# Turning the rounded rows of batches 1 to 7 by VectorE blocks and transfers instead of TensorE

## The reference

```python
def _quant_per_tensor(x):
    scale = max(max(abs(x)), 1e-6) / 127
    return round(x / scale), scale

def _qlinear(x2d, w, b):
    xq, sx = _quant_per_tensor(x2d)
    wq, sw = _quant_per_tensor(w)
    return (xq @ wq.T + b) * (sw * sx)

x = x + tanh(g_xattn) * attention(layernorm(x), ctx)
h = gelu(_qlinear(layernorm(x), w1, b1))      # 512 -> 2048
x = x + tanh(g_ffn) * _qlinear(h, w2, b2)     # 2048 -> 512
```

## Time and profile before

| | |
|---|---|
| median of 3 runs | 369.76 us (368.94 to 369.95) |
| the profiled execution: its own time | 368.73 us |
| its span | 366.9 us |
| TensorE matmuls busy | 349.0 us (95%) |
| VectorE busy | 330.2 us (90%) |
| ScalarE busy | 285.2 us (78%) |
| GpSimd busy | 119.8 us (33%) |
| DMA | 84.78 MB, mean 231 GB/s |

### The profile page before, as it was taken

How to read it: one execution, slowest core, us unless ns; L and a number is a source line. 1 busy time by engine, 2 the same in 40 slices (tenths; PEclk the granted TensorE clock), 3 DMA queues, 4 the chain that set the end, 5 groups by cost and what they waited for, 6 DMA issues and landing times.

```text
span 366.9 us, 6644 instructions
## 1 busy us (share of the span) xinstructions
PE 349.0 (95%) x2406; PEld 245.9 (67%) x2418; DVE 330.2 (90%) x630; ACT 285.2 (78%) x493; POOL 119.8 (33%) x178
## 2 busy tenths in 40 slices
PE   6979989999999888999999999999999999999995
PEld 4667767887886775554545455454548888888884
DVE  3698999999999978999999988987769999999996
ACT  1465879889886965879859988789799999999520
POOL 2644578778689790069000000421000000000000
PEclk9869999999999999999999999999999999999999
DMA  7999978565311463767748760000191999995225
GB/s 222 378 404 403 401 278 280 196 228 216 117 37 80 145 203 128 290 268 312 290 200 341 319 260 0 1 2 0 51 409 56 383 395 424 424 422 233 102 116 229
DMA packets 22963, 84.78 MB, mean 231 GB/s; under 512 B 2129, under 2 KB 11857, under 8 KB 14482
## 3 DMA queue, kind: packets, MB, share of 16 engines
q1 hardware_dynamic: 22272, 83.89, 59.2%
q10 hardware_dynamic: 658, 0.46, 0.4%
HBM read 54.99 MB, written 29.36 MB: 230 GB/s over the span
## 4 chain that ended last, share of the span: by engine, by line
PE 60%; DVE 19%; ACT 10%; issue 5%; DMA 3%; POOL 2%; SPq 1%; DVEq 0%; ACTq 0%; POOLq 0%
PE PS L1460 19%; PE PS L1415 17%; PE PS L1257 7%; DVE hmax L1042 7%; PE PS L1318 6%; ACT ring L703 5%; DMA X<-in_x 3%; PE PS L1299 3%; DVE hmax L832 2%; ACT ring L616 2%; PE PS L1266 2%; PE PS L1312 2%; DVE ring L1019 2%; PE PS L1289 1%; PE PS L1278 1%
## 5 line engine op out<-in xcount | busy, mean ns | idle before, releaser
L683 ACT ACTIVATE ring<-PS,bias,sc 128x512 f32<-128x512 f32 x128 | 97.1, 783 | 21.6 <-PE PS L1415 6.6
L1415 PE MATMUL PS<-mid,w1q 128*128 128x512 bf16 x500 | 110.7, 379 | 1.9 <-DVE mid L996 1.2
L1415 PEld LDWEIGHTS PS<-mid,w1q 128*128 128x128 bf16 x512 | 49.7, 98 | 59.9 <-DVE mid L996 0.7
L1042 DVE TENSOR_REDUCE hmax<-ring 128x1 f32<-128x2048 f32 x30 | 67.4, 2278 | 5.6 <-ACT ring L683 5.6
L703 ACT ACTIVATE ring<-ring,sc 128x2048 int16<-128x2048 f32 x29 | 55.6, 1987 | 0.0
L1460 PE MATMUL PS<-w2q,ring 128*128 128x256 f16 x336 | 39.0, 273 | 0.0
L1257 PE MATMUL PS<-ring 128*128 128x129 f32 x256 | 33.8, 296 | 2.0 <-DVE ring L741 1.5
L1460 PEld LDWEIGHTS PS<-w2q,ring 128*128 128x128 f16 x336 | 32.9, 98 | 4.0
L1257 PEld LDWEIGHTS PS<-ring 128*128 128x128 f32 x256 | 33.0, 212 | 3.1 <-issue 3.1
L1170 DVE SCALAR_TENSOR_TENSOR X<-PS,sc,X 128x512 f32<-128x512 f32 x48 | 35.0, 739 | 0.0
L1318 PEld LDWEIGHTS PS<-w2q,ring 128*128 128x128 f32 x256 | 29.2, 192 | 6.7 <-issue 6.7
(11 more groups left out here) (147 smaller groups left out, 586.8 us busy)
## 6 DMA issues: line engine op xcount, KB each, us to landing
spilled_hidden<-ring SPq DMA_DIRECT2D x20, 1024.0 KB, 3.9
ring<-spilled_hidden SPq DMA_DIRECT2D x20, 1024.0 KB, 9.1
ring<-in_ctxT SPq DMA_DIRECT2D x8, 1024.0 KB, 5.4
ring<-in_ctx SPq DMA_DIRECT2D x8, 896.0 KB, 8.4
X<-in_x SPq DMA_DIRECT2D x7, 1024.0 KB, 9.5
out<-X SPq DMA_DIRECT2D x7, 1024.0 KB, 9.6
ring<-in_w1T SPq DMA_DIRECT2D x4, 1024.0 KB, 13.4
ring<-in_w2T SPq DMA_DIRECT2D x8, 512.0 KB, 3.4
```

Of the source, the lines that this page charges most:

```text
L683: nc.scalar.activation(ring[:, s * CH + c, (h % CH) * N:(h % CH + 1) * N], PS[:, hidden_bank(s, h), :], ACT.Gelu, scale=SC1, bias=bias1[:, ...
L1042: V.tensor_reduce(hmax[:, bass.ds(CH * g + c, 1)], ring[:, s * CH + c, :], AX.X, ALU.max, apply_absolute_value=True).then_inc(hm_done, 1)
L1415: mm = nc.tensor.matmul(PS[:, hidden_bank(s, h), :], w1v[:, k, h * P:(h + 1) * P], xqT[:, s, k, :], start=(k == 0), stop=(k == NH - 1))
```

## The change

For batches 1 to 7 the 16 transposes on TensorE and the two copies from PSUM go. VectorE turns the rounded rows in blocks of 32x32 in place of them (`turn_x`, four instructions of 128x512 for a batch), and SP carries the blocks between the four groups of 32 partitions with 16 transfers of 32 KB (`move`) into `mid`. The matmuls then read the moving operand in runs of 32 columns (`turned_block`). VectorE still rounds batches 1 and 3, both before the w2 maxima; GpSimd rounds batches 2, 4, 5, 6 and 7 (`round_rows`: four scaled subtractions in f32, one addition of a large constant, one subtraction of it with a cast). Batch 2 is rounded ahead of GpSimd's work on w2, the others after it, each once the maxima of group g - 3 are done and its chunks are spilled, since the rows use that slot of `ring`. ScalarE's gelus of group 1 wait until the staging of batches 1 to 3, in the chunks of slot 1, has been read.

```diff
@@ -122,6 +121,26 @@
         S_sb = mid[:, 2048:3072].rearrange("p (j e) -> p j e", e=P)
         xqT = mid[:, :].bitcast(BF16).rearrange("p (s k n) -> p s k n", s=SLOTS, k=NH)
+        xqB = mid[:, :].bitcast(BF16).rearrange("p (s t m) -> p s t m", s=SLOTS, t=NT)
+        def turned_block(g, k):
+            return xqB[:, g % SLOTS].rearrange("p t (k i w) -> p k i t w", k=NH, i=NT)[:, k]
+        def rounded_rows(g):
+            return ring[:, XQ_CHUNK[g], XQ_AT[g]:XQ_AT[g] + CW // 2].bitcast(BF16)
+        def turned_rows(g):
+            return ring[:, T_CHUNK[g], T_AT[g]:T_AT[g] + CW // 2].bitcast(BF16)
+        XQ_CHUNK = [None, 6, 7, 4] + [g % SLOTS * CH + 2 for g in range(4, B)]
+        XQ_AT = [None, 0, 0, 0] + [0] * (B - 4)
+        T_CHUNK = [None, 6, 7, 6] + [g % SLOTS * CH + 2 for g in range(4, B)]
+        T_AT = [None, CW // 2, CW // 2, 0] + [CW // 2] * (B - 4)
+        BY_VECTOR, BY_GPSIMD = (1, 3), (2, 4, 5, 6, 7)
+        TURNED = (1, 3, 2, 4, 5, 6, 7)
         ring16 = ring[:, :, :].bitcast(I16)
...
@@ -368,10 +388,28 @@
                 load_w2(q)
+            def move(g):
+                sp.wait_ge(turned_x, NT * (TURNED.index(g) + 1))
+                if g >= SLOTS:
+                    sp.wait_ge(h_done, KH * (g - SLOTS + 1))
+                for a in range(NT):
+                    for t in range(NT):
+                        sp.dma_start(xqB[32 * a:32 * a + 32, g % SLOTS, t, :],
+                                     turned_rows(g)[32 * t:32 * t + 32, a * D:(a + 1) * D]).then_inc(moved[g], 16)
+            move(1)
             for g in range(SPILLED):
                 for c in range(CH):
+                    if (g, c) == (0, CH - 1):
+                        move(3)
                     sp.wait_ge(gelu_done, KH * g + (c + 1) * KH // CH + len(H_BANK))
                     sp.dma_start(spill[g * CH + c], ring[:, (g % SLOTS) * CH + c, :]).then_inc(spilled[g % SLOTS], 16)
+                if g == 0:
+                    move(2)
+                elif g > 1:
+                    move(g + 2)
+            move(B - 1)
             for p in range(B):
...
@@ -527,6 +565,26 @@
             pool.wait_ge(xs_step, 4)
             nc.gpsimd.tensor_tensor(XROOT, XALL, half[:, 0:1], ALU.pow).then_inc(xs_pow, 1)
+            def round_rows(g):
+                n = BY_GPSIMD.index(g)
+                if g == 2:
+                    pool.wait_ge(mxd_done, B)
+                    pool.wait_ge(rounded_v, 2)
+                else:
+                    pool.wait_ge(spilled[g % SLOTS], 16 * CH * (g // SLOTS) + 1)
+                    pool.wait_ge(hm_done, CH * (g - SLOTS + 1) + 1)
+                pool.wait_ge(xs_step, 8)
+                y = ring[:, 5 if g == 2 else g % SLOTS * CH + 3, :]
+                for i in range(NT):
+                    nc.gpsimd.tensor_scalar(y[:, i * D:(i + 1) * D], X[:, g, i, :], nmean[:, 4 * g + i:4 * g + i + 1],
+                                            rstd[:, 4 * g + i:4 * g + i + 1], ALU.add, ALU.mult).then_inc(rounding_g, 1)
+                pool.wait_ge(rounding_g, (NT + 1) * n + NT)
+                nc.gpsimd.tensor_scalar(y, y, MAGIC, 1.0, ALU.add, ALU.mult).then_inc(rounding_g, 1)
+                pool.wait_ge(rounding_g, (NT + 1) * (n + 1))
+                nc.gpsimd.tensor_scalar(rounded_rows(g), y, -MAGIC, 1.0, ALU.add, ALU.mult).then_inc(rounded_g, 1)
+            round_rows(2)
             pool.wait_ge(w2_step, 8)
...
@@ -536,6 +594,9 @@
                 nc.gpsimd.tensor_scalar(w2q[:, q * CW:(q + 1) * CW], w, -MAGIC, 1.0,
                                         ALU.add, ALU.mult).then_inc(w2q_done, 1)
+            for g in BY_GPSIMD[1:]:
+                round_rows(g)
             pool.wait_ge(w2q_done, CH)
...
@@ -675,8 +736,14 @@
                     if h == 0:
                         act.wait_ge(hm_done, turn * (CH * SLOTS) + 1)
+                    if g == 1 and h == 0:
+                        act.wait_ge(turned_x, 2 * NT)
+                    if g == 1 and h == KH // 4:
+                        act.wait_ge(rounded_g, 1)
                     if g == 1 and h == KH // 2:
-                        act.wait_ge(xT_done, 3)
+                        act.wait_ge(moved[3], 16 * NT * NT)
+                    if g == 1 and h == 3 * KH // 4:
+                        act.wait_ge(moved[2], 16 * NT * NT)
                     if g == 2 and h % (KH // CH) == 0:
...
@@ -1003,30 +1068,27 @@
                 for k in range(1, NH):
                     integers(k)
-            def quantise_x(g, s, turn):
-                if isinstance(g, int) and g == 2:
-                    s = 1
-                    dve.wait_ge(xT_done, 2)
-                    dve.wait_ge(xq_done, 4)
+            def quantise_x(g):
+                n = BY_VECTOR.index(g)
+                dve.wait_ge(xs_step, 8)
+                yt = ring16[:, 4, n * NT * D:(n + 1) * NT * D].rearrange("p (i d) -> p i d", i=NT)
+                for i in range(NT):
+                    V.tensor_scalar(yt[:, i, :], X[:, g, i, :], nmean[:, 4 * g + i:4 * g + i + 1],
+                                    rstd[:, 4 * g + i:4 * g + i + 1], ALU.add, ALU.mult).then_inc(y_done, 1)
+                dve.wait_ge(y_done, 4 * n + 8)
+                V.tensor_copy(rounded_rows(g), yt.rearrange("p i d -> p (i d)")).then_inc(rounded_v, 1)
+            def turn_x(g):
+                if g in BY_VECTOR:
+                    dve.wait_ge(rounded_v, BY_VECTOR.index(g) + 1)
                 else:
-                    dve.wait_ge(spilled[s], 16 * CH * turn + 1)
-                if isinstance(g, int) and g >= SLOTS:
-                    dve.wait_ge(hm_done, CH * (g - SLOTS + 1) + 1)
-                dve.wait_ge(xs_step, 8)
-                yt = ring16[:, s * CH + 3, 0:NT * D].rearrange("p (i d) -> p i d", i=NT)
-                xq = ring[:, s * CH + 2, 0:CW // 2].bitcast(BF16)
+                    dve.wait_ge(rounded_g, BY_GPSIMD.index(g) + 1)
+                rows = rounded_rows(g).rearrange("p (i k a w) -> p i k a w", i=NT, k=NH, w=32)
+                out = turned_rows(g).rearrange("p (a k i w) -> p i k a w", a=NT, k=NH, w=32)
                 for i in range(NT):
...
-            def evacuate(g, s):
-                dve.wait_ge(xT_done, g + 1)
-                for n in range(2):
-                    V.tensor_copy(xqT[:, s, 2 * n:2 * n + 2], psX[:, 2 * n:2 * n + 2]).then_inc(xqT_done, 1)
+                    V.transpose(out[:, i], rows[:, i]).then_inc(turned_x, 1)
             def group_max(g, s, c):
...
@@ -1045,14 +1107,15 @@
             x_scale()
             V.tensor_scalar(rstd[:, :], rstd[:, :], ISX, None, ALU.mult).then_inc(xs_step, 1)
-            quantise_x(1, 1, 0)
-            for k in range(CH - 1):
+            quantise_x(1)
+            turn_x(1)
+            quantise_x(3)
+            turn_x(3)
+            for k in range(CH):
                 w2_max(k)
-            evacuate(1, 1)
-            w2_max(CH - 1)
             dve.wait_ge(w2_step, 4)
             V.tensor_reduce(W2MAX, w2max4, AX.X, ALU.max).then_inc(w2_step, 1)
-            quantise_x(2, 2, 0)
+            turn_x(2)
             dve.wait_ge(w2_all, 1)
...
@@ -1061,14 +1124,10 @@
             V.reciprocal(ISW2, SW2).then_inc(w2_step, 1)
             def group(g, s, turn, last):
-                if g > 1 and not last:
-                    quantise_x(g + 1, (s + 1) % SLOTS, turn + (s + 1) // SLOTS)
                 group_max(g, s, 0)
                 group_max(g, s, 1)
-                if g == 0:
-                    evacuate(2, 2)
-                if g > 1 and not last:
-                    evacuate(g + 1, (s + 1) % SLOTS)
+                if 2 <= g < B - 2:
+                    turn_x(g + 2)
                 group_max(g, s, 2)
...
@@ -1357,20 +1416,6 @@
                 if b >= 0:
                     value_product(b)
-            def transposes(g, s):
...
             pe.sem_inc(gelu_done, len(H_BANK))
...
@@ -1399,21 +1444,20 @@
                 for h in range(KH):
                     if g == 1 and h == 1:
-                        pe.wait_ge(xqT_done, 3)
                         pe.wait_ge(w2_step, 5)
                         across(4, W2MAX).then_inc(w2_all, 1)
-                    if h == (KH // 2 if g == 0 else KH // 4 if g == 1 else 3 * KH // 4) and not last:
-                        if g == 1:
-                            pe.wait_ge(w2_step, 6)
-                        transposes(g + 1, (s + 1) % SLOTS)
                     pe.wait_ge(gelu_done, KH * g + h + 1)
                     for k in range(NH):
                         if h == 0 and g == 0:
                             pe.wait_ge(x0_done, k + 1)
-                        elif h == 0 and k % 2 == 0:
-                            pe.wait_ge(xqT_done, 2 * g + k // 2)
-                        mm = nc.tensor.matmul(PS[:, hidden_bank(s, h), :], w1v[:, k, h * P:(h + 1) * P], xqT[:, s, k, :],
-                                              start=(k == 0), stop=(k == NH - 1))
+                        elif h == 0 and k == 0:
```

(51 more changed lines are left out.)

## The result

The changed kernel takes 397.11 us (median of 4 runs, 396.42 to 397.36) beside 369.35 us for the kernel before on the same chip: a ratio of 1.077 [1.075, 1.079], 27.8 us slower. The forecast was 375.0 us with a range to 384: its sign was right and its size was not.

A forecast was written before the change was run, and what follows sets the result against it. VectorE bounds the stage up to its twelfth maximum, then TensorE for 74 tiles and four transpose blocks. Delays of 3.0 and 2.2 us sum to +5.2: 368.73 becomes 373.9, plus 1.0 for the median, 375.0 us; range 368.5 to 384.

The forecast's parts named there:

- 16 x 0.42 + 3.9 = 10.6 us: SP's move of one batch, last transpose to landing: 16 issues plus one landing; ends 5 and 13.5 us.
- are wanted only by the roundings: SP's queue: spills standing behind moves were said to be needed by nothing except the roundings.
- the upper end 0.60: SP's issue spacing for moves: 0.42 us taken from neighbouring issues 0.42 to 0.60 us apart.
- the eighth maximum at 182.8: VectorE: eight maxima at 2.21 us each, following the w2 scale at 165.1, end at 182.8.
- step 3 and 4: Rounding 4 runs 182.8 to 189.9, twelfth maximum ends 196.8, tile 6 of group 3 starts 6.7 us later; TensorE stands 3.5.
- Steps 1 to 6: The whole schedule, from VectorE's early turns to the loop for batches 5 to 7: stage ends at 263.8 instead of 258.64.
- both stalls: TensorE waits 5.9 us at tile 1 of group 1 for the w2 maximum, and 2.2 us in group 6.
- A: Cheap turns on VectorE: a 512-column transpose costs 0.30 us, giving 367.5 us; chance 0.11.
- C: Dear turns or slow matmuls: a turn of 3.0 us gives 378.2 us, more if dearer; chance 0.12.
- the 1.24 us in proportion: VectorE's transpose of 512 columns scaled from the skill page: 5.0 us a batch, ending near 390 us.
- B: TensorE's clock halves after stalls: 3.07 us lost, swallowed after the first, staying after group 6's; 378.1 us; chance 0.16.
- D: Waits at tile 1 of group 1 and turn 4 do not form; up to 6.2 us gained, 363.6 us; chance 0.02.

The follow-up runs named there:

- one transfer a batch: Changed kernel, each batch's rows moved in one 512 KB transfer instead of 16, without regrouping, so rows lie in wrong places; 375.99 us, ratio 1.020.
- the first run with idle matmuls: Changed kernel with 30, 95, 64 and 28 idle f32 matmuls ahead of four TensorE waits; 414.07 us, ratio 1.123.
- w2 maxima first: Kernel with one transfer a batch, with VectorE's w2 maxima ahead of rounding and turning batch 3; 379.57 us, ratio 1.031.
- five issues: Changed kernel, each batch's turned rows sent to memory in one transfer and back regrouped in four; 381.14 us, ratio 1.034.
- spills by ScalarE: Changed kernel with spills issued by ScalarE, so SP issues only moves in this stage; 388.41 us, ratio 1.054.
- changed, idle matmuls: Changed kernel with 15, 32, 20 and 12 idle f32 matmuls ahead of four TensorE waits, second try; 396.82 us, ratio 1.076.
- 32 transfers: Changed kernel with each of a batch's 16 transfers cut into two of 16 KB, same bytes; 463.03 us, ratio 1.257.

## Why the prediction was wrong

**The failed step** is the term "16 x 0.42 + 3.9 = 10.6 us", put at nothing with +2 as its upper end, with the sentence that the spills behind moves "are wanted only by the roundings". Four things were wrong in it. The pace: an issue of a move costs 0.63 us, 0.83 to 0.93 on average beside spills; the upper end 0.60 came from three issues to another place, with nothing behind them. The list: I let each move start when its rows were turned and counted each alone, where moves 1, 3 and 2 follow one another, with the spills of groups 0 and 1 between and behind them. The word "only": the roundings stand on the very path that the prediction had found to decide. And the gelus: the change itself has ScalarE's gelus of group 1 wait for moves 3 and 2, and the schedule placed the eighth maximum at 182.8 without that wait; it came at 191.12. With the issues few, the other steps give nearly the forecast: the kernel with one transfer a batch takes 375.99 us, 7.3 above its kernel before, where 5.2 were forecast.

How a late rounding reaches the end can be read from seven kernels (not from the first run with idle matmuls, whose longest blocks themselves delay TensorE). Start of GpSimd's rounding of batch 4, and start of TensorE's tile 6 of group 3:

| kernel | rounding 4, us | tile 6, us | difference |
|---|---|---|---|
| one transfer | 182.30 | 197.08 | 14.78 |
| w2 maxima first | 186.77 | 201.56 | 14.79 |
| five issues | 187.42 | 202.22 | 14.80 |
| spills by ScalarE | 192.31 | 207.09 | 14.78 |
| changed, idle matmuls | 195.57 | 210.35 | 14.78 |
| changed | 198.61 | 213.41 | 14.80 |
| 32 transfers | 229.11 | 243.92 | 14.81 |

14.8 us is rounding, turn, two maxima and a gelu, the pass of step 3 and 4, whatever delays its start. The pass of batch 7 is as long: from its rounding to tile 6 of group 6, TensorE's last start after a wait, it takes 14.78 us with one transfer, 14.80 with the second idle matmuls and 14.81 in the changed kernel (249.43 to 264.24). The first of these starts at

```profile
225.98 3.01 POOL L577 TENSOR_SCALAR ring<-X,small 128x512 f32<-128x512 f32 x4 [7.05 <-issue]
```

So the 28.2 us of the stage divide cleanly. 6.4 are there with one transfer a batch (265.07 against 258.64). 23.5 are the later rounding 7 (249.43 against 225.98): 16.3 of them are there at rounding 4 (198.61 against 182.30), the rest is added up to rounding 7, which waits 11.82 us for group 4's spills, issued from 237.53 on behind move 5. And 1.7 come off again, because the last 104 matmuls take 22.62 us, where with one transfer they take 24.31, in part at the lower clock. TensorE's pause of 3.48 us for move 6 and the slow matmuls behind it lie ahead of 264.24 and add nothing: the gelu for which TensorE then waits had itself waited for VectorE's twenty-fourth maximum, which ends at 263.32, 0.08 us before that gelu starts.

**Steps 1 to 6** held in the kernel with one transfer a batch: turn, rounding, both stalls and their places, each within 1.3 us. One size did not: TensorE stands 0.96 us ahead of tile 6 of group 3, not 3.5, because its 148 matmuls behind the first stall take 34.17 us, 2.2 more than at 0.216 each. VectorE sets that tile's start, so nothing came of it.

**Rivals.** A and C fell with the turn's 0.62 us and matmuls at the old pitch. The Trainium skill (VectorE: DVE Perf Modes, The three transpose paths) gives 311 ns for 128 columns; the 1.24 us in proportion that I had from it is not what the trace shows, 0.62 for 512 columns. B came true as a mechanism (a granted clock of 0.50 behind the pause of 8.30 us), but it was not the cause: in the changed kernel its price lies ahead of waits that others end, as the idle matmuls showed. With one transfer a batch it did what B says: the loss after the first stall was swallowed, and the one after the stall in group 6 stayed (24.31 us for 104 matmuls in place of 22.62, at a granted clock of 0.60 from 240.7 to 245.0), 1.7 us where B had 3.07. The Trainium skill (TensorE: Matmul & The Clock Gate, What's actually happening) has the clock go by how busy TensorE has been recently; the trace agrees behind the long pauses. D did not occur.

The rule that I did not weigh speaks against this change: the Trainium skill (DMA: Bandwidth & Descriptors, Rules for kernel authors) says to coalesce many small transfers, since "under 64 KB you're paying mostly overhead". The moves are 32 KB. The trace agrees, and shows which overhead counts here: the landings, 1.9 us each, overlap one another, and SP's issues, 0.63 us each, do not.

**What stays open:** why an issue within the chip's own memory takes 0.63 us for 32 rows, and more beside spills. Only its number, its bytes and, with the one large transfer, its rows were varied.

## What to carry to other kernels

Price a queue as an engine: count its issues, give each a duration from the nearest row and its dearest neighbour, and write its list out in order with start times, as for VectorE; 16 x 7 issues of 0.63 us are 70 us of an engine that "only" starts transfers. For each transfer that slips in that list ask who waits for it, for its landing and for the place that it frees, and whether that one stands on the path already found. And before work is taken off an engine, look at where it is the bound: here the only version that gained moves the transposes of the last three batches, with few issues and with the last turn behind the maximum that others wait for. Batch 4, whose transposes also lie on the chain, was not tried in that way.

## What was not expected of the hardware

A 32 KB transfer of 32 rows within on-chip memory costs its issuer 0.63 us and 16 KB costs 0.64; the 512 KB one of 128 rows costs 0.47. A 32x32-block transpose of 128x512 bf16 takes 0.62 us in a row (0.68 by its own record), near the 0.65 that a reduction of the same width takes in a row (line 811). A moving operand in runs of 32 columns does not slow a matmul (64 in 13.97 us).
